# A layer-norm, attention and int8 feed-forward kernel: masks of neighbouring score groups put behind both groups' products, the quantised product moved behind a pair, opening and finish reordered

## What is computed

```python
q = apply_rope(heads(ln(x) @ Wq)); k = apply_rope(heads(ln(x) @ Wk)); v = heads(ln(x) @ Wv)
scores = q @ repeat(k).T / sqrt(64)                    # causal mask
x = x + (softmax(scores) @ repeat(v)) @ Wo
h = ln(x); scale = max(absmax(h), 1e-7) / 127
qi = clip(round(h / scale), -128, 127)                 # int8, per token
x = x + float16((qi @ weight.T) * scale * w_scale + bias)
```

## Time and profile before

| | us |
|---|---|
| median of 3 runs | 805.92 (805.54 to 808.76) |
| profiled execution, its own time | 809.36 |
| its span in the trace | 807.5 |
| mask of group 0 in step 0 and in step 31 | 56.51 and 765.91 |
| last matmul of the loop's scores | 777.50 |

### The profile page before, as it was taken

One profiled execution on the slowest core, in us unless ns is written; L12 is line 12 of the kernel. 1 busy time (PEld: TensorE's weight loads), 2 busy tenths in 40 slices (PEclk: granted clock), 3 DMA queues, 4 the chain that ended last, 5 costly groups with the idle time before them and its releaser, 6 DMA issues.

```text
span 807.5 us, 23412 instructions
## 1 busy us (share of the span) xinstructions
PE 762.0 (94%) x8230; PEld 641.1 (79%) x8230; DVE 631.9 (78%) x1392; ACT 627.7 (78%) x1731; POOL 572.4 (71%) x526
## 2 busy tenths in 40 slices
PE   3899999999999999999999999999999999999993
PEld 2678888888888887788888888888888887888771
DVE  5757877787878887777778888878788787887886
ACT  4488888788877887788778878888788777887772
POOL 4466877777777886877886887877786887676403
PEclk9799999999999999999999999999999999999995
DMA  8254545564554554554544454455544455354300
GB/s 263 53 124 91 132 112 139 126 153 99 133 125 99 125 122 93 122 117 108 135 114 112 100 127 112 112 125 120 125 106 116 110 117 128 80 119 100 86 2 26
DMA packets 56994, 90.99 MB, mean 113 GB/s; under 512 B 12592, under 2 KB 19248, under 8 KB 56880
## 3 DMA queue, kind: packets, MB, share of 16 engines
q1 hardware_dynamic: 53808, 79.02, 42.5%
q0 software_dynamic: 3072, 10.49, 4.9%
HBM read 16.06 MB, written 2.10 MB: 22 GB/s over the span
## 4 chain that ended last, share of the span: by engine, by line
PE 73%; DVE 8%; ACT 5%; issue 5%; SPq 4%; DMA 4%; POOL 0%; ACTq 0%; POOLq 0%; DVEq 0%
PE x_bank L623 21%; PE t_bank L735 15%; PE o_bank L751 11%; PE s_bank L719 9%; PE s_bank L720 8%; PE s_bank L722 3%; DMA qT<-wv 3%; PE ot_bank L802 3%; ACT prob L1030 2%; PE t_bank L623 2%; DVE probT L1353 2%; SPq L304 2%; SPq L338 1%; DVE o_norm L1388 1%; SPq L342 1%
## 5 line engine op out<-in xcount | busy, mean ns | idle before, releaser
L1030 ACT ACTIVATE prob<-s_bank,neg_max 128x384 f32<-128x384 f32 (+3 forms) x512 | 266.5, 531 | 62.9 <-DVE neg_max L1364 62.8
L1364 DVE TENSOR_REDUCE neg_max<-s_bank 128x1 f32<-128x384 f32 (+3 forms) x352 | 215.9, 636 | 58.3 <-PE s_bank L722 55.5
L1353 DVE SCALAR_TENSOR_TENSOR probT<-t_bank,probT 128x512 f16<-128x512 f32 x320 | 215.5, 682 | 29.5 <-ACT probT L1042 28.7
L1042 ACT ACTIVATE probT<-t_bank 128x512 f16<-128x512 f32 x320 | 189.2, 600 | 43.3 <-PE t_bank L735 38.7
L735 PE MATMUL t_bank<-ident,prob 128*128 128x128 f32 x1280 | 199.1, 278 | 5.0 <-DVE probT L1353 1.4
L719 PE MATMUL s_bank<-kT,qT 128*128 128x384 f32 (+3 forms) x512 | 178.2, 363 | 5.4 <-DMA qT<-wv 3.0
L492 POOL TENSOR_TENSOR wv<-raw,wv 128x512 fp32r<-128x512 f32 x62 | 79.6, 1284 | 132.2 <-ACT wv L991 132.2
L720 PE MATMUL s_bank<-kT,qT 128*128 128x384 f32 (+3 forms) x512 | 157.1, 322 | 0.0
L735 PEld LDWEIGHTS t_bank<-ident,prob 128*128 128x128 f32 x1280 | 137.6, 141 | 14.8 <-ACT prob L1030 7.3
L751 PE MATMUL o_bank<-value,probT 128*128 128x64 f16 x3840 | 138.4, 193 | 0.0
L751 PEld LDWEIGHTS o_bank<-value,probT 128*128 128x128 f16 x3840 | 131.4, 98 | 6.0
(11 more groups left out here) (123 smaller groups left out, 954.4 us busy)
## 6 DMA issues: line engine op xcount, KB each, us to landing
qT<-wv SPq DMA_DIRECT2D x248, 128.0 KB, 2.4
swp<-raw SPq DMA_DIRECT2D x320, 64.0 KB, 2.0
kT<-key_pair SPq DMA_DIRECT2D x128, 128.0 KB, 2.4
wg_raw<-in_w_group POOLq DMA_DIRECT2D x16, 384.0 KB, 4.8
wg_raw<-in_w_group POOLq DMA_DIRECT2D x16, 256.0 KB, 3.8
resid<-in_x SPq DMA_DIRECT2D x4, 512.0 KB, 8.7
out<-resid SPq DMA_DIRECT2D x16, 128.0 KB, 2.1
wo_stage<-in_w_out SPq DMA_DIRECT2D x4, 256.0 KB, 3.0
```

Of the source, the lines that this page charges most:

```text
L1030: nc.scalar.activation(prob[:, slot:slot + blocks, h, :], s_bank[G % SCORE_BANKS][:, at * n:(at + 1) * n].rearrange("p (k n) -> p k n", n= ...
L1042: nc.scalar.activation(turned_half[B % TURNED][HI], t_bank[B % TURN_BANKS][:, :], ACT.Copy, scale=PROB_SCALE).then_inc(probT_hi, 1)
L1353: nc.vector.scalar_tensor_tensor(out=turned_half[B % TURNED][LO], in0=t_bank[B % TURN_BANKS][:, :], scalar=PROB_SCALE, in1=turned_half[B % ...
L1364: nc.vector.tensor_reduce(neg_max[:, s % 2, u:u + len(heads)], s_bank[G % SCORE_BANKS][:, 0:len(heads) * n].rearrange("p (h n) -> p h n", ...
```

## The change

Four things move; no instruction of the loop is added or dropped.

1. `scores` is cut in `score_products` and `score_mask`, and `score_pair(s, a)` gives the products of groups `a` and `a + 1` and then their two masks. Pairs are (4, 5), (8, 9) and, for the coming step, (1, 2).
2. `ffn_product` moves from between groups 8 and 9 to behind the pair, on DVE `scale_product` from before `keep_probT_low(s, 3)` to behind `maxima(s, 9)`.
3. Opening: `project(1, 0)` goes right behind the first key projection, ahead of the value products; `wg[1]`'s high part is copied by ACT and not by POOL; on DVE the low parts of the value weights come before the statistics of batch 1, and `value_low`, `keep_xT_low` and the statistics are interleaved in another way, with `cast_ffn_weights` and `rotate_first(0, 1)` later.
4. Finish: `normalise_output(31, 3)` comes one add and one statistics earlier; the last four tiles take their roots in two and two and not in three and one; tile 14 is normalised by ACT and not by POOL, and tile 13 rounded to whole numbers by ACT and not by DVE.

```diff
-            def scores(s, a):
+            def score_products(s, a):
...
+            def score_mask(s, a):
+                if not inside(s):
+                    return
...
                 nc.tensor.matmul(diagonals, ident_b[:, :], mask[:, :].unsqueeze(1).broadcast_to([P, len(heads), P]),
                                  start=False, stop=True, skip_group_check=True).then_inc(scores_done, 1)
+
+            def scores(s, a):
+                score_products(s, a)
+                score_mask(s, a)
+
+            def score_pair(s, a):
+
+                score_products(s, a)
+                score_products(s, a + 1)
+                score_mask(s, a)
+                score_mask(s, a + 1)
...
             project_keys(0)
+            project(1, 0)
             values(0)
+            values(1)
+            values(2)
+            spread_power()
             turn_xn(4)
-            values(1)
-            spread_power()
+            values(3)
             turn_xn(5)
-            values(2)
             turn_xn(6)
-            values(3)
-            project(1, 0)
+            values(4)
             turn_xn(7)
-            values(4)
...
                 turn(s, 0)
-                scores(s, 4)
-                scores(s, 5)
+                score_pair(s, 4)
                 project_keys(s + 2)
...
-                scores(s, 8)
+                score_pair(s, 8)
                 ffn_product(done_tile(s))
-                scores(s, 9)
                 turn_output(s, 0)
...
                 attend(s, 9)
-                scores(s + 1, 1)
-                scores(s + 1, 2)
+                score_pair(s + 1, 1)
                 out_product(s, 2)
...
-            cast_ffn_weights()
+            keep_wv_low(0)
+            keep_wv_low(1)
             dve.wait_ge(x_loaded[1], 16)
...
                 maxima(s, 8)
-                scale_product(done_tile(s))
                 keep_probT_low(s, 3)
                 batch_statistics(s, 1)
                 maxima(s, 9)
+                scale_product(done_tile(s))
                 keep_probT_low(s, 4)
...
+                if s == STEPS - 1:
+                    normalise_output(s, 3)
+                    aggregate(LOOP_TILES, LOOP_TILES + 2, TOK_TILES)
+                    add_eps(3, slice(LOOP_TILES, LOOP_TILES + 2))
                 add_product(s, 2)
                 last_statistics(s, 2)
```

More of the change, by code:

```diff
@@ L43 @@
 LAST_TILE = TOK_TILES - 1
-ACT_TILE = LOOP_TILES + 1
 ROOT_BITS = float(0x5F3759DF)
@@ L917, in value_magnitudes, with keep_group_weights @@
                     nc.scalar.activation(wv_abs[k], wv_raw[k], ACT.Abs).then_inc(wv_abs_done, 1)
-            def keep_first_weights():
-                act.wait_ge(wg_loaded[0], 16)
-                nc.scalar.activation(wg[0][:, HI, :, :], wg_raw[0][:, :, :], ACT.Copy).then_inc(wg_hi, 1)
+            def keep_group_weights(n):
+                act.wait_ge(wg_loaded[n], 16)
+                nc.scalar.activation(wg[n][:, HI, :, :], wg_raw[n][:, :, :], ACT.Copy).then_inc(wg_hi, 1)
             def keep_wv(k):
@@ L1065, in _ @@
             keep_xT(3)
+            keep_group_weights(1)
             keep_raw(0, 0)
+            keep_raw(0, 1)
             keep_wv(0)
             keep_wv(1)
-            keep_raw(0, 1)
             keep_raw_keys(0)
+            keep_value(0)
             root(1, slice(Q_TILES, 2 * Q_TILES))
+            keep_value(1)
             normalise(4)
             normalise(5)
+            keep_value(2)
+            keep_xT(4)
             normalise(6)
             normalise(7)
-            keep_value(0)
-            keep_xT(4)
-            keep_value(1)
             keep_high(0, 0)
+            keep_value(3)
             keep_xT(5)
-            keep_value(2)
             keep_xT(6)
-            keep_value(3)
+            keep_value(4)
             root(2, slice(2 * Q_TILES, TOK_TILES))
@@ L1126, in _ @@
             for s in range(STEPS + 1):
-                if s == STEPS:
-                    root(3, slice(LOOP_TILES, LAST_TILE))
                 exponentials(s, 1, 0)
@@ L1164, in _ @@
                 to_whole(done_tile(s + 1))
-                if s == STEPS:
-                    normalise_done(ACT_TILE)
-                    root(4, slice(LAST_TILE, TOK_TILES))
                 keep_oT(s, 2)
+                if s == STEPS - 1:
+                    root(3, slice(LOOP_TILES, LOOP_TILES + 2))
                 keep_raw(s + 2, 1)
@@ L1171, in _ @@
                     exponentials(s + 1, 0, h)
+            normalise_done(LOOP_TILES + 1)
+            root(4, slice(LOOP_TILES + 2, TOK_TILES))
             round_tile(LOOP_TILES)
             to_whole(LOOP_TILES)
-            for f in range(LOOP_TILES + 1, TOK_TILES):
-                round_tile(f)
+            normalise_done(LOOP_TILES + 2)
+            round_tile(LOOP_TILES + 1)
+            to_whole(LOOP_TILES + 1)
+            round_tile(LOOP_TILES + 2)
+            round_tile(LAST_TILE)
         @block.vector
@@ L1475, in _ @@
             for s in range(STEPS + 1):
-                normalise_output(s - 1, 3)
-                if s == STEPS:
-                    aggregate(LOOP_TILES, LAST_TILE, TOK_TILES)
-                    add_eps(3, slice(LOOP_TILES, LAST_TILE))
+                if s < STEPS:
+                    normalise_output(s - 1, 3)
                 maxima(s, 3)
@@ L1538, in _ @@
             done_statistics(last)
-            aggregate(last, last + 1, TOK_TILES)
-            add_eps(4, slice(last, last + 1))
+            aggregate(LOOP_TILES + 2, TOK_TILES, TOK_TILES)
+            add_eps(4, slice(LOOP_TILES + 2, TOK_TILES))
+            absolute_maximum(LOOP_TILES + 1)
             absolute_maximum(LOOP_TILES)
-            absolute_maximum(LOOP_TILES + 1)
             scale_inputs((LOOP_TILES, LOOP_TILES + 1))
-            finish_root(4, slice(last, last + 1))
+            finish_root(4, slice(LOOP_TILES + 2, TOK_TILES))
+            offset_means(4, slice(LOOP_TILES + 2, LOOP_TILES + 3))
             dve.wait_ge(out_ready, last % LOOP_TILES + 1)
@@ L1547, in _ @@
                                     ALU.subtract, ALU.mult).then_inc(last_xn_done, 1)
+            absolute_maximum(last)
             absolute_maximum(LOOP_TILES + 2)
-            absolute_maximum(last)
             scale_inputs((LOOP_TILES + 2, last))
             keep_quant(LOOP_TILES)
-            to_whole(LOOP_TILES + 1)
+            keep_quant(LOOP_TILES + 1)
             to_whole(LOOP_TILES + 2)
             scale_product(LOOP_TILES)
-            keep_quant(LOOP_TILES + 1)
             to_whole(last)
+            scale_product(LOOP_TILES + 1)
             keep_quant(LOOP_TILES + 2)
-            scale_product(LOOP_TILES + 1)
             keep_quant(last)
```

58 lines of the change are left out of this document (31 added, 27 removed).

## The result

The changed kernel takes **849.59 us** (median of 4 runs, 846.56 to 851.57), the kernel before 807.34 (4 runs, 805.54 to 810.15). The ratio is 1.0517, with a 95% interval from 1.0488 to 1.0545: 5.2% slower. The forecast was 845 us.

A forecast was written before the change was run, and what follows sets the result against it. PE was taken as the bound nearly everywhere, ACT for a stretch of every odd step. Terms summed to +28.8 us, giving 834.7 us; clock falls of +10.2 made it 845 us, range 823 to 857.

The forecast's parts named there:

- the late mask: Early pairs: first mask behind both groups' products delays DVE's maximum and ACT's exponential; exp(1,0) 0.43 us late, exp(1,3) 0.58.
- the held projection: Eleven steps: scale_product, later on DVE, frees x_bank later, so project(s+2,0) starts 1.94 us later than now.
- pairs (1,2) and (4,5): Loop, early score groups: late masks cost +9.3 us over odd steps and +2.4 us over even steps.
- pair (8,9), quantised product in step 30: Late loop: pair saves 1.3 us over 20 steps without a quantised tile; step 30, without the projection, saves 0.4.
- projection held, without the clock: Eleven steps with a quantised tile: project(s+2,0) 1.94 us later each, +21.3 us, clock falls not counted.
- opening: Before the loop: project(1,0) fills PE's 3.57 us wait, partly lost to other waits; -1 us, from -4 to +4.
- finish: End of kernel: normalise_output(31,3) earlier removes PE's 1.30 us wait, root cut 2 and 2; -1.5 us, from -2.5 to 0.
- clock: Behind the new projection waits: granted clock falls in about six of eleven, 1.7 us lost each, +10.2 us.
- the early pairs are free: Rival, early score groups: unseen DVE or ACT slack, 11.7 us less, 823 without and 833 with the clock; chance 0.10.
- The saving of 0.08: PE, each pair: second group's products follow a product instead of a mask, saving 0.08 us; 7.7 us if all counted.
- PE waits there instead: Opening: tiles 8 to 11 are turned only once DVE has all statistics, a counterweight within the -1 us taken.
- clock holds: Rival, loop: the granted clock stays full through the projection waits, 835 us (828 to 841); chance 0.29.

The follow-up runs named there:

- e1: The changed kernel with scale_product back before keep_probT_low(3) on DVE; 816.48 us, ratio 1.0127 to the kernel before.
- e2: As e1, with pairs (1,2) and (4,5) also undone and pair (8,9) kept; 805.27 us, ratio 0.9986 to the kernel before.
- e7: The kernel before with pair (8,9) and the quantised product behind it, scale_product in its old place; 807.53 us, ratio 1.0009.
- e4: The changed kernel with 36 unread bf16 matmuls added before project(s+2,0) in eleven steps; 834.72 us, ratio 1.0350 to the kernel before.
- e8: The kernel before with only scale_product moved behind maxima(9) on DVE; 832.95 us, ratio 1.0326.
- e10: The kernel before with pair (8,9), the quantised product behind it, and scale_product between the maxima of groups 7 and 8; 806.94 us, ratio 0.9996.

## Why the prediction was right, point by point

The time was within 0.6% of the forecast, and the two mechanisms that make the loss, the late mask and the held projection, were the ones forecast. That the sum came so near is luck in part, for errors of several microseconds cancel in it. The terms, from the runs:

| term | forecast us | measured us | from |
|---|---|---|---|
| pairs (1,2) and (4,5) | +11.7 | +11.2 | e1 less e2 |
| pair (8,9), quantised product in step 30 | -1.7 | about 0 | e7 |
| projection held, without the clock | +21.3 | +18.2 (traces: +21.1) | e4 less e1 |
| opening | -1.0 | about 0 | first masks |
| finish | -1.5 | -2.0 | from the last mask on |
| clock | +10.2 | +14.9 | the change less e4 |

With the 18.2 the right-hand column adds up to the measured 42.3 us (three of its terms are differences between neighbours in one chain of kernels); the forecast's column gives 39.0.

**Early pairs: right.** ACT waits for neg_max before exp(1,0), which comes 0.40 us late (forecast 0.43), and `turn(1)` 0.52 late (forecast 0.58); 126 waits of ACT where there were 63. In an odd step nothing of the 0.08 us that a pair saves on PE was left, since PE would have waited for ACT anyway. The rival that said the early pairs are free is out: each of them costs time alone. What makes 0.52 us of them in an odd step is pair (4,5), and the bank of group 2 through which pair (1,2) delays it further; pair (1,2) alone moves `turn(1)` by 0.09.

**A mask behind a mask.** In step 15 the two masks of a pair and the start of what follows take 0.10 us with pair (1,2) (417.01 to 417.11) and 0.13 with pair (4,5), so about 0.05 each, as taken. The Trainium skill's 81 ns for each short matmul in a stream ("TensorE: Matmul & The Clock Gate", section "Back-to-back issue gap") is too long for these two masks; the trace decides, and nothing in the sum hung on it.

The saving of 0.08 was right too for pair (1,2): its second group's first product is followed after 0.24, where it was 0.32. In pair (4,5) the first product of group 5 still waits for its bank and takes 0.28, so less was saved there.

**The projection: the right size, by a working that hid a second bound.** `project(s+2,0)` was forecast to wait 2.38 us beyond its usual distance from `turn(4)`; it is 2.42. With PE's order left alone (e8) it is 2.05 to 2.09 us late, where 1.94 was forecast: the sum let it start 0.04 us behind the end of `scale_product`, and it starts 0.15 behind. The other error is larger. The prediction read the earlier trace rows as "the projection starts without a wait". It missed that the gap was held by `scale_product` at the same instant. For the change it made no difference, since the later place of `scale_product` overrode both. In e7's and e2's expectations it was most of the first error (6.6 us of gain expected, none found) and about half of the second (9 us): 11 x 0.44 = 4.8 us counted as a gain that the second bound had already taken. The step that failed in them is the overlap: a gain on PE was booked without asking when `scale_product`, which kept its place, would let go of x_bank. It ends 0.14 to 0.15 us ahead of the projection in before, e7, e10 and the change alike.

**Pair (8,9): mis-sized.** -1.3 us was taken; e7 shows nothing. Measured at the projection, it is a loss of 0.02 to 0.06 in even steps, and in seven of nine odd ones a gain of 0.06 to 0.09 on PE, of which, in some steps, a wait in front of group 0 of the next step takes a part.

**Opening: only by luck near.** The first wait is gone, as foreseen, and a longer one stands elsewhere:

```profile
36.90 0.69 PE L613 MATMUL s_bank<-ident,probT 128*128 128x128 f32 x2 [5.03 <-ACT probT L945]
...
34.00:40.00 6.00, 3.10 (x9) 2.41 (x10) 3.17 (x10) 3.95 (x9) 1.28 (x1) 0.50 0.00 0
```

PE waits 5.03 us for a tile that ACT normalises (L945) before it can turn it; the same wait was 1.5 us before. The granted clock is now at half from 33.8 to 40.6 us, where it was from 23.0 to 33.2. This is the mechanism that was weighed against the gain ("PE waits there instead"); it took all of it and not two thirds. The earlier trace rows was also no fair sample: of the seven traces with the old opening only that one has a wait as long as 3.57 us before the first value product (the others 1.95 us or less) and 10 us of half clock. Five have none at all, and e8 has 3.4 us. All six traces with the new opening have the wait of 5.03 us, and 6.8 us of half clock that begins inside it.

**Finish: right.** `turn_output(31, 3)` starts at 831.35 with no wait in front, where it had 1.30.

**The clock: the term that was too small.** Eight falls and not six, each 1.9 us and not 1.7. The length at half clock was right (3.4 us; 3.5 taken), by luck: the 3.5 was a third of the opening's 10 us, and no row had shown it. The rival "clock holds" gave 835; e4 shows that time, 834.7, with PE kept busy, but the rest of the sum meets it only because its errors cancel: 3 us too much for the projection in the medians, against nearly 3 us of gain from pair (8,9) and the opening that did not come. Gaps of 2.2 us brought the clock down eight times in eleven in the trace of the change, and gaps of 1.8 us four times in eleven in that of e8. The Trainium skill (same page, section "Why this matters for your kernels") warns of long idle gaps between bursts of matmuls; in these two traces short ones were enough.

What stays open: why the eleven waits of one length bring a fall in some steps and not in others. The runs show how many, not which, and how many in one traced execution of each kernel only. The two early pairs cost 11.2 us together by the medians of e1 and e2 and 9.4 in the loop of their traces; the openings of the two traced executions differ by another 4.2 us (55.81 and 51.57), which no edit explains.

## What to carry to other kernels

- A start without a printed wait does not mean a single bound. Before a gain is booked on one chain, follow every other thing that the instruction needs and see when it was ready. Where it was ready no earlier than the usual hand-over ahead of the start (0.15 us here), the gain is zero until both move.
- When a step is moved on the engine that reads a shared bank, price the bank's next user and not the moved step: 0.47 us of DVE's work moved by two places cost 18 to 21 us in waits and about 15 more in clock.
- When two delays are taken alone and together, and don't add up, look for a buffer that ties them: here about 3 of 11 us came from one pair's late exponential holding the other's bank.
- A row of one execution is a sample. The opening's wait and its half clock were in one trace of seven.
- To take the clock's part out of a loss, fill the wait with products that nobody reads. If the wait stays and the time falls, the difference is the clock.

## What the runs showed of the hardware

- The 2.4 GHz level was lost behind single waits of 2.2 us (eight of eleven, the change) and of 1.8 us (four of eleven, e8), in one traced execution each and in a loop that is dense on both sides. It fell between PE's return and 1.5 us after it (once 0.2 us before the return), and the half clock lasted some 3.4 us each time, at 1.9 us of lost time.
- In the opening it fell during a wait of 5.03 us in six traces of six; with waits of at most 1.95 us it stayed at full in five of six.
- 36 bf16 products of 128 columns ran in 2.17 us, 0.06 us each, and held the clock at full through every one of these waits.
- From the end of DVE's read of a bank to the next start on PE it is 0.14 to 0.15 us in the traces of four kernels; from the issue of a short product on PE to DVE's start on its result it is 0.42 us.
